# Order of work and the engine of one copy between the GRU stack and the FFN of a one-core kernel

## The reference

```python
x = x + _L0_xcond_ref(_layernorm(x), ctx_1024, cond_1024, ..., L0_xcond_fusion_W, L0_xcond_fusion_b, ...)
x = x + _L0_ffn_ref(_layernorm(x), L0_ffn_W_fc, L0_ffn_ln_w, L0_ffn_ln_b, L0_ffn_W_proj)

def _L0_ffn_ref(x, W_fc, ln_w, ln_b, W_proj):
    h = jnp.einsum('btd,hd->bth', x, absmean(W_fc))
    h = jax.nn.gelu(h, approximate=False)
    h = layernorm(h, ln_w, ln_b)
    return jnp.einsum('bth,dh->btd', h, absmean(W_proj))
```

## Time and profile before

| | us |
|---|---|
| median of 3 runs (lowest, highest) | 1667.66 (1667.36, 1669.31) |
| the profiled execution | 1667.05 |
| its span | 1665.3 |
| TensorE busy | 1565.3 (94%) |
| VectorE busy | 1403.4 (84%) |
| GpSimd busy | 1129.4 (68%) |
| ScalarE busy | 1003.6 (60%) |
| granted clock of TensorE, mean over the span | 0.984 |

### The profile page before, as it was taken

The page is one execution under the profiler, slowest core; times in us unless marked ns, Lnnn a source line. Parts: engine busy times, 40 slices in busy tenths (PEclk is TensorE's granted clock), DMA queues, the critical chain, the costliest instruction groups (busy, mean ns, idle before and its releaser), DMA issues.

```text
span 1665.3 us, 23148 instructions
## 1 busy us (share of the span) xinstructions
PE 1565.3 (94%) x7794; PEld 1282.6 (77%) x7794; DVE 1403.4 (84%) x2171; ACT 1003.6 (60%) x1663; POOL 1129.4 (68%) x1029
## 2 busy tenths in 40 slices
PE   5899999989999999999899789999999999999997
PEld 4677887877878778787788678888788787878876
DVE  6977999998999989999888865888887979797866
ACT  6677878888677887787887222434444343344344
POOL 5666776878979779887799632555555656465545
PEclk9999999999999999999999988999999999999999
DMA  4011131312312011212034421020202111111000
GB/s 158 8 64 63 40 114 52 127 64 91 112 38 83 33 55 61 89 62 104 32 133 152 166 94 39 20 82 20 82 20 67 35 57 45 57 45 57 8 19 32
DMA packets 72282, 111.62 MB, mean 67 GB/s; under 512 B 5091, under 2 KB 37859, under 8 KB 69094
## 3 DMA queue, kind: packets, MB, share of 16 engines
q1 hardware_dynamic: 72166, 110.15, 19.4%
HBM read 72.38 MB, written 37.75 MB: 66 GB/s over the span
## 4 chain that ended last, share of the span: by engine, by line
PE 59%; POOL 14%; DVE 11%; ACT 8%; issue 7%; DMA 0%; DVEq 0%; POOLq 0%; SPq 0%; ACTq 0%
PE ps L454 15%; PE ps L540 13%; PE ps L558 13%; PE ps L507 10%; POOL hb L1409 5%; POOL H L1418 4%; PE ps L488 3%; PE ps L474 3%; DVE bnp L1020 2%; ACT ntok L764 2%; POOL rsp L1430 2%; ACT hb L753 1%; DVE H L1008 1%; DVE AL L1037 1%; DVE H L1009 1%
## 5 line engine op out<-in xcount | busy, mean ns | idle before, releaser
L454 PE MATMUL ps<-AH,WH 128*128 128x512 f32 x896 | 368.6, 411 | 15.2 <-DVE H L1009 9.4
L1409 POOL TENSOR_TENSOR hb<-zb,hb 128x512 f32<-128x512 f32 x224 | 290.0, 1295 | 107.1 <-ACT hb L753 106.7
L454 PE MATMUL ps<-AL,WH 128*128 128x512 f32 x896 | 352.2, 393 | 0.0
L454 PE MATMUL ps<-AH,WL 128*128 128x512 f32 x896 | 351.1, 392 | 0.0
L1513 POOL TENSOR_TENSOR acq<-acq,sq 128x512 f32<-128x512 f32 x120 | 180.0, 1500 | 184.9 <-ACT sq L860 184.9
L851 ACT ACTIVATE g<-ps 128x512 f32<-128x512 f32 x128 | 76.7, 599 | 322.7 <-PE ps L540 322.7
L1000 DVE TENSOR_TENSOR_SCAN zb<-ps,hb 128x512 f32<-128x512 f32 x192 | 234.3, 1220 | 38.1 <-POOL hb L1409 35.0
L1418 POOL TENSOR_TENSOR H<-H,zb 128x512 f32<-128x512 f32 x192 | 248.3, 1293 | 14.2 <-DVE zb L1000 11.5
L1183 DVE SCALAR_TENSOR_TENSOR gl<-g,wcol,gh 128x512 fp32r<-128x512 f32 x128 | 123.8, 967 | 127.5 <-ACT gh L857 127.5
L1197 DVE TENSOR_TENSOR acc<-acc,g 128x512 f32<-128x512 f32 x120 | 212.3, 1769 | 0.0
L454 PEld LDWEIGHTS ps<-AH,WH 128*128 128x128 f32 x896 | 169.6, 189 | 52.5 <-DVE H L1009 12.8
(11 more groups left out here) (137 smaller groups left out, 3377.0 us busy)
## 6 DMA issues: line engine op xcount, KB each, us to landing
hs_scratch<-H SPq DMA_DIRECT2D x16, 1024.0 KB, 5.6
hc<-hs_scratch SPq DMA_DIRECT2D x32, 512.0 KB, 4.3
xr<-in_x SPq DMA_DIRECT2D x32, 256.0 KB, 4.4
out<-ob SPq DMA_DIRECT2D x32, 256.0 KB, 2.2
xbuf<-in_x SPq DMA_DIRECT2D x7, 1024.0 KB, 7.8
RAW<-in_wt SPq DMA_DIRECT2D x16, 256.0 KB, 6.6
stg<-in_fct SPq DMA_DIRECT2D x16, 256.0 KB, 3.6
stg<-in_pjt SPq DMA_DIRECT2D x16, 256.0 KB, 2.6
```

Of the source, the lines that this page charges most:

```text
L454: r = e.matmul(GATE[i % 3][:], w[:, q, m * 128:(m + 1) * 128], a[:, q, :], start=(n == 0), stop=(n == 11))
L1409: e.tensor_tensor(hb[c][:], zb[c][:], hb[c][:], ALU.mult).then_inc(s_p, 1)
```

## The change

- **TensorE, seam.** Order before: fuse(0), fuse(1), tokens(LAST), feat(0), fuse(2), feat(1), fuse(3), feat(2), feat(3), then the loop. After: fuse(0), fuse(1), feat(0), fuse(2), feat(1), fuse(3), feat(2), tokens(LAST), columns(0), feat(3), columns(1), then the loop. `USERS` follows it. The 64 small products move from j = 3 to there, in two halves of 32, and write to PS[2] in place of TURNED. fuse(4, 0) waits for sum_columns in place of feat(4); proj(0) waits also for stats(LAST).
- **The copy hch** goes from VectorE (in `cut`) to ScalarE (`whole`), with its waits for the load, for the buffer (f_fu) and, for unit 0, for job 54's matmuls. whole(0) stands in slot 57 between gates 2 and 3 of job 54; whole(1) to whole(3) behind the slots; whole(4) behind unit_feat(3); from then on one in every step with c = 3, 6, 9, 12, behind hidden(j).
- **VectorE, seam.** cut(2) before unit_norm(0), cut(3) before unit_lo(0), columns() between resid(2,0) and resid(2,1), stats(LAST) behind unit_norm(3), sum_columns() before cut(4) and the loop.
- **GpSimd.** addx(0) in slot 58 before the adds of jobs; inv_1(2), addx(3), inv_1(3) before inv(LAST).

```diff
--- before.py
+++ after.py
@@ -153,9 +153,8 @@
             USERS += [("T", _i, _n, 0), ("T", _i, _n, 1)]
         elif _i is not None and (_who == "x" or TAILS[_i][2] < 3):
             USERS.append(("x" if _who == "x" else "h", _i, _n))
-USERS += [("F", _u, _h) for _u in (0, 1) for _h in (0, 1)]
+USERS += [("F", _u, _h) for _u in range(4) for _h in (0, 1)]
 USERS += [("T", LAST, _n, _i) for _n in (0, 1) for _i in (0, 1)]
-USERS += [("F", _u, _h) for _u in (2, 3) for _h in (0, 1)]
 BANK = {u: n for n, u in enumerate(USERS)}
 T1N = {u: n for n, u in enumerate(u for u in USERS if u[0] == "T")}
 T2N = {u: n for n, u in enumerate(u for u in USERS if u[0] in "xh")}
@@ -499,6 +498,7 @@
                 e.wait_ge(d_fu, 32)
             if u == 4 and h == 0:
                 e.wait_ge(s_sc, 4 * NJ)
+                e.wait_ge(f_cs, 1)
             if u == 7:
                 e.wait_ge(f_cbo, 2)
             n = 0
@@ -516,8 +516,6 @@
                 e.wait_ge(f_xh, u)
             if u >= 8 and u % 4 == 0:
                 e.wait_ge(f_vg, u // 4 - 1)
-            if u == 4:
-                e.wait_ge(f_cs, 1)
             if u == 6:
                 e.wait_ge(f_cbo, 2)
             for m in range(KC):
@@ -551,6 +549,7 @@
                 e.wait_ge(d_pj[c // 4], 16)
             if j == 0:
                 e.wait_ge(f_x1, 8)
+                e.wait_ge(s_bs, 2 * STATS[("h", LAST, 1)])
             for t in range(4):
                 if b > 0 and c == 0:
                     e.wait_ge(f_ev, 4 * b - 3 + t)
@@ -571,16 +570,16 @@
                 r = e.matmul(TURNED[:, 4 + t:5 + t], acq[b % 2][:, t * 128:(t + 1) * 128], ones[:], start=True, stop=True)
             r.then_inc(f_st, 1)
 
-        def columns():
-
-            e.wait_ge(f_bl, 2)
-            for i in range(4):
-                e.wait_ge(d_pj[i], 16)
-            e.wait_ge(f_xh, 4)
-            e.wait_ge(f_xl, 4)
-            for m in range(KC):
+        def columns(h):
+
+            if h == 0:
+                e.wait_ge(f_bl, 2)
+                e.wait_ge(s_sc, 4 * NJ)
+                for i in range(4):
+                    e.wait_ge(d_pj[i], 16)
+            for m in (2 * h, 2 * h + 1):
                 for k in range(NC):
-                    r = e.matmul(TURNED[:, 4 * m:4 * m + 4], PJ[k][:, m * 128:(m + 1) * 128], wb[:, k, :], start=(k == 0),
+                    r = e.matmul(PS[2][:, 4 * m:4 * m + 4], PJ[k][:, m * 128:(m + 1) * 128], wb[:, k, :], start=(k == 0),
                                  stop=(k == NC - 1))
             r.then_inc(f_cc, 1)
 
@@ -690,8 +689,6 @@
         fuse(0, 1)
         fuse(1, 0)
         fuse(1, 1)
-        tokens(LAST, 0)
-        tokens(LAST, 1)
         feat(0)
         fuse(2, 0)
         fuse(2, 1)
@@ -699,7 +696,11 @@
         fuse(3, 0)
         fuse(3, 1)
         feat(2)
+        tokens(LAST, 0)
+        tokens(LAST, 1)
+        columns(0)
         feat(3)
+        columns(1)
         for j in range(NB * NC):
             b, c = j // NC, j % NC
             fc(j)
@@ -711,8 +712,6 @@
                 fuse(4 * b + 4 + FUSE_AT.index(c - 1), 1)
             if j >= 2:
                 proj(j - 2)
-            if j == 3:
-                columns()
             if j == 10:
                 spread()
             if b + 1 < NB and c - 3 in FUSE_AT:
@@ -828,6 +827,16 @@
             if ABS0 <= s < ABS0 + 16:
                 absolute(2 * (s - ABS0))
                 absolute(2 * (s - ABS0) + 1)
+
+        def whole(u):
+
+            i = u % 2
+            e.wait_ge(d_hc[i], 16 * (u // 2) + 16)
+            if u >= 2:
+                e.wait_ge(f_fu, 2 * u - 2)
+            if u == 0:
+                e.wait_ge(s_mm, 4 * JOB[(7, 0, 3)] + 4)
+            e.activation(hch[i][:], hc[i][:], ACT.Copy).then_inc(f_sh, 1)
 
         def unit_feat(u):
 
@@ -938,6 +947,8 @@
             feature("h", tail(s - 4), 3)
             feature("x", batch(s - 1), 3)
             gates(job(s - 2), 2)
+            if s == 57:
+                whole(0)
             norm_x(batch(s))
             gates(job(s - 2), 3)
             if s == 7:
@@ -959,8 +970,14 @@
                 take_rows(1)
             feature("h", tail(s - 3), 2)
 
-        for u in range(4):
-            unit_feat(u)
+        whole(1)
+        whole(2)
+        whole(3)
+        unit_feat(0)
+        unit_feat(1)
+        unit_feat(2)
+        unit_feat(3)
+        whole(4)
         for j in range(NB * NC):
             b, c = j // NC, j % NC
             hidden(j)
@@ -973,6 +990,8 @@
                     e.activation((c1, cB)[i][:], p[:], ACT.Copy).then_inc(f_cbo, 1)
             if b + 1 < NB and c - 3 in FUSE_AT:
                 unit_feat(4 * b + 4 + FUSE_AT.index(c - 3))
+            if c - 1 in FUSE_AT and 4 * b + 5 + FUSE_AT.index(c - 1) < NU:
+                whole(4 * b + 5 + FUSE_AT.index(c - 1))
         for t in range(4):
             evacuate(NU - 4 + t)
 
@@ -1117,12 +1136,6 @@
         def cut(u):
 
             i = u % 2
-            e.wait_ge(d_hc[i], 16 * (u // 2) + 16)
-            if u >= 2:
-                e.wait_ge(f_fu, 2 * u - 2)
-            if u == 0:
-                e.wait_ge(s_mm, 4 * JOB[(7, 0, 3)] + 4)
-            e.tensor_copy(hch[i][:], hc[i][:]).then_inc(f_sh, 1)
             e.wait_ge(f_sh, u + 1)
             e.tensor_tensor(hcl[i][:], hc[i][:], hch[i][:].bitcast(F32), ALU.subtract).then_inc(f_sp, 1)
 
@@ -1205,8 +1218,8 @@
                 e.tensor_tensor(wb[:, :, 2 * i + 1], v[:], wb[:, :, 2 * i].bitcast(F32), ALU.subtract).then_inc(f_bl, 1)
 
         def sum_columns():
-            e.wait_ge(f_cc, 1)
-            e.tensor_copy(cbc[:], TURNED[:, 0:4 * KC].rearrange("p (m i) -> p m i", i=4)).then_inc(f_l0, 1)
+            e.wait_ge(f_cc, 2)
+            e.tensor_copy(cbc[:], PS[2][:, 0:4 * KC].rearrange("p (m i) -> p m i", i=4)).then_inc(f_l0, 1)
             e.wait_ge(f_l0, 1)
             c_v = cbc[:].rearrange("p m (v i) -> p v m i", v=2)
             e.tensor_tensor(rows[:], c_v[:, :, :, 0], c_v[:, :, :, 1], ALU.add).then_inc(f_cs, 1)
@@ -1349,16 +1362,15 @@
             stats(tail_b(s - 2), 0)
         resid(0, 0)
         resid(0, 1)
+        cut(2)
         unit_norm(0)
-        cut(2)
         resid(1, 0)
         resid(1, 1)
+        cut(3)
         unit_lo(0)
         unit_norm(1)
-        stats(LAST, 0)
-        stats(LAST, 1)
-        cut(3)
         resid(2, 0)
+        columns()
         resid(2, 1)
         unit_lo(1)
         unit_norm(2)
@@ -1366,8 +1378,10 @@
         resid(3, 1)
         unit_lo(2)
         unit_norm(3)
+        stats(LAST, 0)
+        stats(LAST, 1)
         unit_lo(3)
-        columns()
+        sum_columns()
         cut(4)
         for j in range(NB * NC):
             b, c = j // NC, j % NC
@@ -1375,8 +1389,6 @@
                 deviation(b - 1)
             low_part(j)
             total(j)
-            if j == 4:
-                sum_columns()
             if b + 1 < NB and c in FUSE_AT:
                 resid(4 * b + 4 + FUSE_AT.index(c), 0)
             if b + 1 < NB and c - 1 in FUSE_AT:
@@ -1587,6 +1599,8 @@
             inv_x(batch(s + 1))
             value(job(s - 2), 2)
             inv(tail(s - 3), 0)
+            if s == 58:
+                addx(0)
             inv(tail_b(s - 4), 1)
             add(job(s - 2), 1)
             value(job(s - 2), 3)
@@ -1597,19 +1611,17 @@
             add(job(s - 2), 3)
             value(job(s - 1), 1)
             add(job(s - 1), 0)
-            if s == 58:
-                addx(0)
             aside(s)
 
         addx(1)
         inv_1(0)
         addx(2)
         inv_1(1)
+        inv_1(2)
+        addx(3)
+        inv_1(3)
         inv(LAST, 0)
         inv(LAST, 1)
-        addx(3)
-        inv_1(2)
-        inv_1(3)
         addx(4)
         for j in range(NB * NC):
             b, c = j // NC, j % NC
```

## The result

| | before | changed |
|---|---|---|
| median of 4 runs | 1667.76 us | 1644.47 us (1643.98 to 1644.74) |
| ratio | | 0.9855, 95% interval 0.9844 to 0.9867 |
| profiled execution, its span | 1667.05, 1665.3 us | 1644.74, 1642.9 us |

The change takes off 23.3 us. The forecast was 1648.3 us, range 1640.5 to 1655: right in direction and range, 3.8 us too little gained.

A forecast was written before the change was run, and what follows sets the result against it. The seam was taken as bound by hand-overs between engines and the clock they cost, not TensorE's work. 6.5 + 10.85 + 2.1 = 19.4 us off 1667.05 gave 1647.65, as a median 1648.3 us, range 1640.5 to 1655.

The forecast's parts named there:

- Part 1: Ahead of the seam: without the copy hch on VectorE, fuse(0,0) starts 0.7 us earlier, bounds 0 to 0.7.
- Part 2: Seam, TensorE's new order: first fc 6.5 us earlier, old products' place saves 10.85, low clock over fc 2.1; 19.4 us.
- The products: Seam: 64 small products at their new place take 10.8 us, low clock after about 3 us; feat(3) takes 0.6.
- Part 3: Units 4 to 31: the copy's move to ScalarE gains 0; bounds 3.8 us gained, 2 us lost.
- the prediction's own last sign: After 1020 us: the prediction is wrong if that stage changes by more than 3 us.
- the sign "unchanged": Later stage, 1020 to 1590: TensorE's six waits for n1, 3.8 us in all, stay unchanged.
- PJ loads: Seam: the four loads the products need are issued some 4 us earlier and land near 953, needed at 960.
- A: Seam: the clock stays full through the products, 26.2 us gained, so 1641.5 us; chance 12%.
- B: Seam: the clock falls earlier, all from the transposes on at half, 4.5 us worse: 1652.8 us; chance 20%.
- C: Seam: VectorE becomes the bound of units 1 to 3, 5.2 us over four units: 1653.5 us; chance 12%.
- D: Steady stage: late ScalarE copies stop feat in each of 28 units; with 1.0 us each 1676 us; chance 3%.
- E: Seam: another late hand-over eats most of the gain, within 0.2% (2%) or something between (1%); chance 3%.

The follow-up runs named there:

- copy_on_vectore: The changed kernel with the copy hch back on VectorE inside cut, all orders kept: 1650.82 us, ratio 0.9897 to the kernel before.
- order_only: The kernel before with only the orders of the change, the copy on VectorE and the products at j = 3: 1655.75 us, ratio 0.9929.
- steady_copy_only: The kernel before with only the copy hch moved to ScalarE for units 5 to 31, seam untouched: 1663.53 us, ratio 0.9972.

## Why the prediction was right, and where it was off

- **Part 1** (0.7 us ahead of the seam, bounds 0 to 0.7): 1.71 us, outside the bounds. The step took away the copy's 0.69 us and left hcl at 2.20 as a fixed price. Without the copy hcl starts before GpSimd's add, at 927.12 against 927.46, and no longer behind it:

```profile
927.12 1.22 DVE L1140 TENSOR_TENSOR hcl<-hc,hch 128x1024 fp32r<-128x1024 f32 x1
928.26 1.22 DVE L1019 TENSOR_TENSOR_SCAN zb<-ps,hb 128x512 f32<-128x512 f32 x1
```

  1.22 us in place of 2.20, and the whole wait of 1.7 us is gone. copy_on_vectore brings it back. The way from mm(55,0) to fuse(0,0) is 13.0 us in every trace with the first copies on ScalarE and 14.7 in the four that have them on VectorE (before, copy_on_vectore, order_only, steady_copy_only).
- **Part 2, the path to the first fc.** Predicted 36.35 us from fuse(0,0) (21.9 + 1.05 + 1.6 + 0.4 + 10.8 + 0.6), measured 37.07. The wait for feat(0) was 1.3, not 0.4: hcl was taken with its neighbour's price, the inverse root (1.54) not. Units 2 and 3 had no wait, as said; the fourth bank of the transposes neither.
- **The products** with feat(3), forecast as 10.8 and 0.6 us with 28 at full clock: 10.64 us, from 963.23 to 973.87, with 32 at full clock. The low clock over the first fc: 7.32 us for the three (before 7.52), where the sum had put 5.45 + 2.8, the loss of the old place. That is the 0.9 us by which the way from the first fc to feat(4) gained more than forecast (13.84 against 10.85 + 2.1).
- **Part 3, the later stage**, taken at 0, bound 3.8: 4.9 us. This step failed, and alone it is more than the 3.8 us that the forecast missed. By the prediction's own last sign, a change of more than 3 us after 1020, it was wrong here. It looked at the one wait that was listed six times (n1 at c = 14), argued that VectorE waits for gh in c = 13 anyway, and took that for the whole stage. VectorE does wait there, and still 0.2 us a batch were won on that wait (six waits of 3.8 us became 2.5), against the sign "unchanged". The wait that mattered more was another, the second half of the fusion for the residual addition, 0.33 us each at c = 6 and c = 9, which the waits list once, with 0.4 us. The cost of ScalarE's pass was right: 1.04 us, no idle time before it in the later stage, and VectorE is never idle ahead of hcl. ScalarE's groups, 1020 to 1570:

```profile
L869 ACT ACTIVATE sq<-g 128x512 f32<-128x512 f32 x104 | 64.3, 618 | 13.1 <-POOL acq L1525 13.1
L860 ACT ACTIVATE g<-ps 128x512 f32<-128x512 f32 x105 | 62.9, 599 | 233.4 <-PE ps L538 233.4
L839 ACT ACTIVATE hch<-hc 128x1024 fp32r<-128x1024 f32 x25 | 26.1, 1044 | 0.0
```

- **PJ loads**: landed in time. The fourth was issued at 944.9 and landed 12.7 us later, at 957.6 (the text said near 953), 5.6 us before the first product.
- **Rivals.** A (clock stays full) is excluded: it fell in every trace, in the changed kernel after 32 products at 1.00. B (low from the transposes on): no, the transposes and 32 products ran at 1.00. The Trainium skill's sentence that transposes don't count as a busy TensorE ("TensorE: Matmul & The Clock Gate", Part 4: PE-mode transpose) is neither shown nor excluded: the clock held for 6.3 us of transposes and small products and then fell, and all twelve traces have the same 20 transposes behind fuse(3). C (VectorE as the bound of units 1 to 3): no, order_only has the copies on VectorE and units 2 and 3 without waits. D: no, the later stage became faster by 4.9 us. E: no, the only late hand-over is the 1.3 us ahead of feat(0).
- **The ledger.** 1.0 us more in part 1, 0.7 less on the way to the first fc, 0.9 more behind it, 4.9 more later, 3.1 less through the execution's own start; 19.4 + 1.0 - 0.7 + 0.9 + 4.9 - 3.1 = 22.4 us, the difference of the two spans. That the number came so near is in part luck: no step foresaw the 3.1 us of the start, and without them the two traces differ by 25.5 us, against 19.4 forecast. The execution would have been some 1641.6 us, still in the range, but at its lower end, where the prediction had put rival A.

## What to carry to other kernels

A list of waits names what came last, and leaves out short ones: to cost an operation that leaves a queue, compare the length of the repeated steps, and look at every place where the bottleneck's engine takes a result of that queue, a PSUM bank freed as well as an operand made. Order is worth more than fewer instructions where an engine's queue has a waiting instruction ahead of ready ones; filler work in a hole is worth about the hole (here 4.2 us of waits, and 5 to 6.5 us measured, a part of which is clock). Removing one wait of the seam did nothing measurable alone. Before a saving of 1 or 2 us is put down to an edit, compare how long the clock was low in both traces.

## What the runs showed of the hardware

- ScalarE's copy of 128x1024 fp32 from SBUF takes 1.04 us, its square of 128x512 0.62 (changed kernel): 0.42 us for 512 elements more, which leaves 0.2 fixed, an estimate from two different functions. VectorE's copy took 0.68 to 0.70 us, and once, in copy_on_vectore at 939.31 beside GpSimd's work, 1.19 (order_only has one of 1.18).
- In the changed kernel GpSimd's inverse root of one column takes 0.55 us at its shortest and 1.47 to 1.54 beside VectorE's hcl; VectorE's n1 0.54 at its shortest and 1.49 beside a GpSimd addition (947.70).
- After the last matmul of fuse(3) the clock fell from 2.4 to 1.2 GHz after 5.4 to 8.2 us in the twelve traces of the new order, whether 64, 32, 4 or no products stood behind the transposes; it stayed low for 3.4 to 13.7 us. In two executions of the changed kernel it fell after 6.3 and 6.5 us. In the two traces of the old order (before, steady_copy_only), with a wait of 3.7 us behind fuse(3), it fell after 4.3. This alone moves an execution by a few microseconds, as much as the smaller edits here.
- In the last batch the clock fell once more for 3.4 us, between 1572 and 1600, in eight of the fourteen traces; the batch then took 79.2 to 80.1 us, in the other six 77.9 to 78.9.
